# A limit of two transfers under way on the scatters that sort tokens to experts

## What is computed

```python
x = x + 0.5 * ffn(layernorm(x))
x = x + attention(layernorm(x))     # 16 heads, causal
x = x + 0.5 * ffn(layernorm(x))

# ffn, for N = 2048 tokens, E = 32 experts, K = 4
shared = silu(xf @ sg) * (xf @ su) @ sd
...                                  # scores, top 4 of 8 groups, top 4 experts, gates
capacity = int(N / E * K * 1.25)     # 320 rows of each expert
pos = cumsum(onehot)[token, expert] - 1
keep = pos < capacity
buf[expert, pos] = xf[token]         # where keep; each token goes to 4 experts
h = silu(buf @ wg) * (buf @ wu)
out_e = h @ wd
routed[token] += out_e[expert, pos] * gate * keep
```

## Time and profile before

| | us |
|---|---|
| measured, median of 3 | 1134.17 |
| measured, lowest and highest | 1133.24, 1136.13 |
| profiled execution, span from first to last instruction | 1172.3 |
| profiled execution's own time beyond the span | not recorded |
| TensorE (PE) busy in it | 972.9 (83%) |
| VectorE (DVE), ScalarE (ACT), GpSimd (POOL) busy | 548.8, 356.1, 365.8 |
| the 128 scatters (L451) on POOL | 124.6, mean 974 ns |
| mean granted clock of TensorE | 0.945 |

### The profile page before, as it was taken

One profiled execution on the slowest core, in us unless ns is written; L12 is line 12 of the kernel. 1 busy time (PEld: TensorE's weight loads), 2 busy tenths in 40 slices (PEclk: granted clock), 3 DMA queues, 4 the chain that ended last, 5 costly groups with the idle time before them and its releaser, 6 DMA issues.

```text
span 1172.3 us, 17171 instructions
## 1 busy us (share of the span) xinstructions
PE 972.9 (83%) x5887; PEld 752.4 (64%) x5887; DVE 548.8 (47%) x1503; ACT 356.1 (30%) x701; POOL 365.8 (31%) x550
## 2 busy tenths in 40 slices
PE   2305699999198999999999999999999653999994
PEld 1203366666134888979888498887999632666663
DVE  7533244444536674727273556362712541444444
ACT  2100122222023335343432443434353210222222
POOL 2736435555100311111110011444421073355551
PEclk9998899999579999999999999999999775999997
DMA  9400234453400000000000000101000002344435
GB/s 362 166 24 27 58 93 142 146 164 99 147 18 0 19 1 19 1 19 1 19 1 1 0 20 1 37 20 38 19 1 1 28 27 58 105 142 147 153 96 183
DMA packets 79285, 76.31 MB, mean 65 GB/s; under 512 B 10409, under 2 KB 69947, under 8 KB 78454
## 3 DMA queue, kind: packets, MB, share of 16 engines
q1 hardware_dynamic: 70006, 63.15, 17.3%
q0 software_dynamic: 9216, 12.33, 3.1%
HBM read 48.13 MB, written 30.21 MB: 67 GB/s over the span
## 4 chain that ended last, share of the span: by engine, by line
PE 72%; DVE 10%; issue 7%; another core or an unknown queue 6%; DMA 2%; ACT 2%; SPq 1%; POOL 1%; DVEq 0%; POOLq 0%; ACTq 0%
PE PS L1232 22%; PE PS L1143 8%; PE PS L1212 7%; PE PS L1129 6%; PE PS L1194 6%; PE PS L1130 5%; PE PS L1174 3%; PE PS L1283 3%; PE PS L1151 2%; PE PS L1197 1%; PE PS L1176 1%; PE PS L1109 1%; PE PS L1267 1%; DVE xs L899 1%
## 5 line engine op out<-in xcount | busy, mean ns | idle before, releaser
L1232 PE MATMUL PS<-area_v,pT 128*128 128x128 f32 x2304 | 316.5, 277 | 2.9 <-POOL pT L463 2.9
L1232 PEld LDWEIGHTS PS<-area_v,pT 128*128 128x128 f32 x2304 | 305.3, 192 | 13.3 <-POOL pT L463 3.0
L605 ACT ACTIVATE pT<-PS 128x512 f32<-128x512 f32 (+3 forms) x384 | 185.1, 490 | 250.6 <-PE PS L1212 244.8
L463 POOL TENSOR_SCALAR_AFFINE_SELECT pT<-pT 128x128 f32<-128x128 f32 x256 | 78.7, 311 | 469.4 <-ACT pT L605 468.3
L917 DVE TENSOR_REDUCE mxp<-PS 128x2 f32<-128x1024 f32 (+2 forms) x192 | 180.6, 955 | 83.0 <-PE PS L1197 62.2
L482 POOL DMA_INDIRECT ybuf<-area_o,yidx x160 | 155.4, 971 | 184.1 <-DVE area_o L876 143.3
L451 POOL DMA_INDIRECT xbuf<-xn,sidx x128 | 124.6, 974 | 130.6 <-DVE sidx L812 67.0
L1212 PE MATMUL PS<-Qc,Kz 128*128 128x512 f32 (+3 forms) x384 | 156.4, 411 | 7.8 <-ACT pT L605 5.3
L1143 PE MATMUL PS<-area_v,area_o 128*128 128x128 f32 (+1 forms) x768 | 126.5, 291 | 0.0
L1194 PE MATMUL PS<-Kz,Qn 128*128 128x512 f32 (+3 forms) x384 | 117.9, 389 | 4.1 <-DVE mxp L917 3.3
L1143 PEld LDWEIGHTS PS<-area_v,area_o 128*128 128x128 f32 (+1 forms) x768 | 93.9, 172 | 31.8 <-issue 11.3
(11 more groups left out here) (172 smaller groups left out, 945.1 us busy)
## 6 DMA issues: line engine op xcount, KB each, us to landing
area_v<-xbuf SPq DMA_DIRECT2D x32, 340.0 KB
area_v<-in_L_ffn_wg_dram SPq DMA_DIRECT2D x32, 256.0 KB
area_v<-in_L_ffn_wu_dram SPq DMA_DIRECT2D x32, 256.0 KB
area_v<-in_L_ffn_wd_dram SPq DMA_DIRECT2D x64, 128.0 KB
yg<-ybuf SPq DMA_DIRECT2D x24, 256.0 KB, 4.4
xbuf<-Kz SPq DMA_DIRECT2D x4, 1360.0 KB, 10.3
ybuf<-Kz SPq DMA_DIRECT2D x2, 2048.0 KB
Kz<-Kn SPq DMA_DIRECT2D x32, 128.0 KB
```

The costliest lines, as they stand in the source:

```text
L463: nc.gpsimd.affine_select(out=block_, in_=block_, pattern=[[1, P]], compare_op=ALU.is_ge, fill=zero, base=0, channel_multiplier=-1).then_i ...
L605: nc.scalar.activation(pT[:, N % 4, 0:w], PS[:, 4 + N % 2, 0:w], ACT.Exp).then_inc(exp_done, 1)
L1232: ins = mm(PS[:, 6 + half, (i % 4) * P:(i % 4 + 1) * P], pT[:, N % 4, k * P:(k + 1) * P], area_v[:, (j * NH + h) * VW:(j * NH + h) * VW + ...
```

## The change

The one semaphore `scat` becomes two. Scatters are numbered through both layers, and number n adds to `scat[n % 2]`. In `scatter` every transfer from the third on waits before it is sent until all earlier ones of its own parity have landed, the latest of which is the second last one. The scatters that stand between attention's mask operations get the number and the semaphore, but no wait. Who waited for all scatters of a layer now waits on both semaphores.

```diff
-        scat = sem("scat")
+        scat = [sem(f"scat{k}") for k in range(2)]
...
-                sp.wait_ge(scat, 64 * 16 * (L + 1))
+                for k in range(2):
+                    sp.wait_ge(scat[k], 32 * 16 * (L + 1))
...
                 for t in range(lo, hi):
                     for k in range(K):
+                        sent = scatter_number(L, H, t, k)
+                        if sent >= 2:
+                            pool.wait_ge(scat[sent % 2], 16 * (sent // 2))
                         scatter_one(L, H, t, k)
+
+            def scatter_number(L, H, t, k):
+                return ((2 * L + H) * HT + t) * K + k
...
-                    xn[:, H * HT + t, :], None, bounds_check=SLOTS - 1, oob_is_err=False).then_inc(scat, 16)
+                    xn[:, H * HT + t, :], None, bounds_check=SLOTS - 1, oob_is_err=False)\
+                    .then_inc(scat[scatter_number(L, H, t, k) % 2], 16)
...
-                    dve.wait_ge(scat, 64 * 16)
+                    for k in range(2):
+                        dve.wait_ge(scat[k], 32 * 16)
```

## The result

| | us | ratio to the kernel before on the same chip |
|---|---|---|
| kernel before, this comparison | 1134.41 (1133.24 to 1136.13) | |
| changed kernel | 1165.23 (1164.61 to 1171.5) | 1.0288 [1.0261, 1.0315] |
| changed kernel, profiled execution | span 1162.9, own time 1164.61 | |

The change makes the kernel slower, by 30.8 us between the medians and 32.7 by the ratio. The direction and the place were forecast. The size was not: the sum gave 20.6 us, and 1134.17 x 1.0288 = 1166.8 lies just above the range's end of 1166. The interval of the ratio, 1163.8 to 1169.9, has that end inside it.

The account below looks back on a forecast made before the run. The prediction took POOL's scatter run, which the experts wait for, as the bound. Layer 0's 15.4 us (start 4.9 plus 30 pairs at 0.35) and layer 1's 5.2 made 20.6: 1134.2 + 20.6 = 1154.8 us, range 1138 to 1166.

Parts of the forecast that it names:

- What bounds the kernel: In both layers the experts wait for POOL's scatter run, so every us added to the scatters is in the open.
- The reconstruction of the unstalled execution: Stalls taken out of layer 0: second scatter run ends 20.2 us earlier, experts' first transpose starts near 119 instead of 148.50.
- belongs to the recording: Engines' standstill beside the scatter runs comes from profiling; measured runs have nearly none; about 40 us against a 38.1 gap.
- The wait is open, and costs landing plus waking: In POOL's scatter runs, two scatters take landing 2.2 plus release to start 0.86, against 2.55 us before.
- the wait is hidden: Rival: in the scatter runs two scatters stay at 2.55 and only the start costs; 1139 us, chance 0.18.
- nothing on the path: Rival: the shared expert ends after the scatters in both layers, hiding the delay; 1134 or up to 3 more, chance 0.06.
- I count one too many, so I take 2.9: Scatter pair in both layers: 3.06 cut to 2.9 for a waking counted twice, 0.35 us more than 2.55.
- the forecast's 10.5: Layer 0's scatters from number 2 to 63: the limit adds 10.5 us, at 0.35 a pair.
- layer 1's steps: Layer 1's late scatter run: 15 pairs at 0.35 us more each, 5.2 us.
- The start: Layer 0's first run: number 2 waits for number 0, landing at about 38.0, and starts 4.9 us later.
- nothing more is charged: TensorE's clock ahead of the experts: TensorE stood idle there before and does after, so no added time.
- the stalls are the machine's and the limit lifts them: Rival: standstills beside the scatter runs are real and go, 29.5 + 11 us off, 20.6 on; 1114 us, chance 0.07.

Follow-up runs that it names:

- before_again: The kernel before, unchanged, profiled once more on chip C, a chip of the lower level: own time 1133.33 us, span 1131.6.
- before_less8: The kernel before without its last 8 scatters of layer 0, measuring time only: 1122.08 us, ratio 0.9899.
- free_start_again: The changed kernel with the limit only from number 8 on, second run, on chip D: 1161.75 us, ratio 0.9928 to the kernel before.
- pace288: The kernel before, no limit, with a 128x288 GpSimd memset behind each of 96 scatters: 1155.88 us, ratio 0.9873, on chip E.
- depth8: The changed kernel with eight semaphores, each scatter waiting for the eighth last: 1174.38 us, ratio 0.9999 to the kernel before, on chip A.

## Why the prediction was right or wrong

**What bounds the kernel: right.** POOL's scatter run is what the experts wait for. The chains of before_again and of the changed kernel show it in both layers, before_less8 by experiment in layer 0. The reconstruction of the unstalled execution was within 1.4 us at both points, at the second with luck.

**The standstill "belongs to the recording": wrong.** Recording alone does not bring the 38.1 us between the span and the median. before_again was recorded too and has no such piece, and on chips A, D and E the 17 to 29 timed runs of the kernel before, each with a span some 1.75 us under its time, are 36 to 41 us above those of the lower level. The profile and the times on record were of two levels. One thing the record can't settle: the opening has the measured times as taken without the profiler, but each timed run of these comparisons comes with a span and a granted clock, and the own time of the profiled execution is one of the measured times (1164.61). So it is not shown that the standstill would be there with the recorder off, only that the recorder runs without it on chips B and C. The Trainium skill (NOTIFIC — the notification-queue block, section 7.1) has a rule by which recording can hold an engine back; no run here shows it at work, and it does not explain why chips B and C have none of these pieces. The conclusion drawn from the step, that the measured runs have no standstill, was true of the first comparison all the same, so the base of the sum stood. That was luck: on a chip of the upper level the same reasoning would have met 0.9983 and not 1.0288.

**The wait is open, and costs landing plus waking: right in kind.** The rivals "the wait is hidden" (1139) and "nothing on the path" (1134) are out. From a landing to the start of the scatter that waits for it the chain after shows 0.79 us. The Trainium skill (DMA: Bandwidth & Descriptors, section "Anatomy of one DMA — SWDGE (gpsimd) path") gives some 50 ns for the sequencer's dispatch, and the measurement decides against a price of that size. The same section's fit for one transfer, 2.0 us plus the bytes over 436 GB/s, gives an estimate of 2.16 for 128 x 136 x 4 bytes; the runs here nearly agree with it, 2.30 with all rows and 2.17 with some out of bounds.

**The step that failed: "I count one too many, so I take 2.9".** The sum of the two rows, 3.06, was right and the deduction was not: next to nothing of the 2.20 was SP's own waking, since the landing by itself takes 2.18 at the end of both runs of before_again. It takes 2.30 with all rows going out and 2.17 at the end, and a pair 3.09 falling to 2.92. Over layer 0 a pair is (94.97 - 2.1) / 30.5 = 3.045. With that the 61 steps cost 30.5 x (3.045 - 2.552) = 15.0. One late landing adds 2.1, and 0.7 us of irregular steps that the kernel before had there go off: 16.4, which is 5.9 us above the forecast's 10.5. In layer 1 the same error is hidden by another one: before_again loses 1.1 us between its first two late scatters, so the term came out at 5.6 against 5.2. The pair is the largest part of the miss but not all of it. Of the 10.7 us between 31.3 and 20.6 it makes 4.5 in layer 0; the late landing less the irregular steps makes 1.4, the start 0.8, layer 1's steps 0.4, and what the sum left out 3.6. With 3.06 for a pair the sum would have been 4.9 + 45 x 0.51 = 27.9 and the time 1162.

**The start: right, 5.7 us against 4.9.** Number 0 lands at 39.00, not 38.0. With number 2 waiting for it the DMA engines are still full with the hardware queue; free_start_again confirms the term with 6.1.

**What the sum left out: 3.6 us net in four places.** Two of them have a cause that rows suggest. Ahead of layer 1's first late scatter POOL takes 2.40 us of "issue":

```profile
929.22 0.19 DVE sidx L821
929.55 2.40 issue
...
932.17 0.99 POOL xbuf L458
```

In before_again a gap of the same kind stands one scatter later (906.93 to 909.33). It looks like one break in POOL's program that has moved, and it costs 1.9 here where it cost 1.1 there. What it is no row says. The second is the clock, for which the prediction has "nothing more is charged". TensorE waits 34.75 us ahead of `turn` in layer 0 in place of 12.45, and the first 10 us of the experts are granted 0.50 in place of 0.58, that is 1.2 GHz throughout (stretches of the changed kernel and of before_again, both from some 2 us ahead of `turn`):

```profile
138.00:148.00 10.00, 6.92 (x16) 4.60 (x17) 1.75 (x7) 1.58 (x3) 0.00 (x0) 0.50 0.51 150
```

```profile
116.40:126.40 10.00, 6.98 (x18) 4.53 (x19) 1.75 (x7) 1.70 (x4) 0.00 (x0) 0.58 0.51 148
```

From the first transposition to the load of `yg` the changed kernel takes 159.51 us and before_again 158.54. That this 1.0 us is the clock is argued, not shown.

**The rival "the stalls are the machine's and the limit lifts them", given 0.07: half of it is real.** On chips of the upper level the limit does lift them. The reason that the rival gives, that fewer outstanding scatters leave the other engines' semaphores and fetches free, no run shows. But the price is 31 us and not 20.6, so what comes out is 0.9983, no gain to speak of. It would have been the likeliest case had the times on record come from such a chip. The objection made against it, that at 1.276 fewer than two are under way so that the limit changes nothing but the pace, was correct, and the pace is what counts (pace288).

**Still open:** what stands still, and why on some chips only. The chain names no releaser for these pieces, and no run changed the chip's part in it. One trace has a lead that nothing here follows up. In the trace of the kernel before, both long pieces (from 46.50 and from 956.41) begin about 1 us after a packet of an instruction queue starts, and depth8 has such a packet in 46:46.3 and a piece from 47.19. The rows of the DMA queues in the trace of the kernel before, for 45.3 to 45.6 and for 955.3 to 955.6 us:

```profile
q14 instruction: 1, 0.01, 9.3%
...
q8 instruction: 1, 0.02, 25.8%
```

before_again has such a packet in 45.6:46 as well and no standstill, so the packet alone does not bring it.

## What to carry to other kernels

A limit on transfers under way does not change the pace as long as limit x pace is longer than landing + waking (here 3 x 1.276 = 3.83 against 3.09). Once it is shorter, as with 2 x 1.276 = 2.55, charge every pair the full sum of both. Either way charge the first wait by the landing that it really meets, which in a stretch of full DMA queues is several times longer (7.60 against 2.30). Where a span is longer than the measured times, take a second profile on another chip before giving the difference to the recorder: here it went with a level of time that three of the five chips had in every run. And where engines stand still beside a long run of transfers from POOL, spacing the transfers by some instruction of POOL (pace288) is a cheaper test than waiting for landings, and at the upper level it was the cheaper remedy. At the lower level there is nothing to remedy, and it only costs (22 us by the estimate above).

## What the runs showed of the hardware that was not expected

- With indirect transfers from POOL every 1.276 us, the other engines stand still for up to 29 us at a time on three of five chips, and not on the two others. With limits of 3 and 8 it is still there (64.5 and 75.1 us of unnamed pieces); at 1.49 apart it is gone. The level of a chip was the same in all of its runs of the kernel before (1166.92 to 1180.83 in 71 runs on A, D and E, 1131.19 to 1136.33 in 24 on B and C).
- A wait on POOL ahead of an indirect transfer delays it 0.79 us behind the release, and none of it is hidden behind the transfer before; a wait already met costs nothing (steps of 1.275 with it in depth8 against 1.276 without).
- A memset of 0.17 us between two indirect transfers costs 0.02 us a step, because it runs in the 0.30 us gap that is there anyway; one of 0.36 us costs 0.21.
